# Row maxima turned and loaded in two halves of the heads, scores three slots later, three stacks in place of four

## The reference

```python
h = concat(pos_table, nest_table[nesting(x)], seg_table[segments(x)]) @ W      # (32, 512, 128)
n = layernorm(h)
q, k, v = heads(n @ qkv_w.T + qkv_b)                # 8 heads of 16
h = h + (softmax(q @ k.T / 4) @ v) @ out_w.T + out_b
n = layernorm(h)
g = softmax(n @ gate_w.T) - sigmoid(n @ thr_w.T) / 4
w = where(g >= 0, g, 0); w = w / sum(w)             # 4 experts
h = h + sum_e w_e * (((relu(n @ fc1_e.T) @ loraA_e) @ loraB_e) @ fc2_e.T)
```

## Time and profile before

| | |
|---|---|
| median of three runs | 1129.23 us (1129.39, 1129.23, 1126.67) |
| the profiled execution | 1126.86 us, span 1125.1 us |
| PE busy (matmuls, ends modelled) | 1040.1 us, 92% of the span |
| DVE busy | 948.8 us, 84% |
| ACT busy | 807.0 us, 72% |
| POOL busy | 682.1 us, 61% |
| 1024 maxima tiles on DVE (L1025) | 649.0 us, 679 ns each |
| 1024 exponentials on ACT (L592) | 556.3 us, 600 ns each |
| mean granted TensorE clock | 0.962 of 2.4 GHz |

### The profile page before, as it was taken

One profiled execution on the slowest core, in us unless ns is written; L12 is line 12 of the kernel. 1 busy time (PEld: TensorE's weight loads), 2 busy tenths in 40 slices (PEclk: granted clock), 3 DMA queues, 4 the chain that ended last, 5 costly groups with the idle time before them and its releaser, 6 DMA issues.

```text
span 1125.1 us, 20263 instructions
## 1 busy us (share of the span) xinstructions
PE 1040.1 (92%) x6158; PEld 407.9 (36%) x6158; DVE 948.8 (84%) x2442; ACT 807.0 (72%) x1578; POOL 682.1 (61%) x684
## 2 busy tenths in 40 slices
PE   4368999999999999999999999999999999989865
PEld 2112233333434434343433443434343343333322
DVE  7498899999989989899999999999999998887312
ACT  2217787777877788787877778778787777856731
POOL 1855676677666666677666666667766666621231
PEclk9558999999999999999999999999999999999997
DMA  2553645555554445555555545565555554541111
GB/s 74 148 135 89 137 106 135 129 137 127 137 130 124 126 121 130 142 127 134 126 137 126 126 121 132 130 143 126 137 125 137 128 126 113 121 96 36 55 50 32
DMA packets 93530, 132.43 MB, mean 118 GB/s; under 512 B 18205, under 2 KB 69918, under 8 KB 87398
## 3 DMA queue, kind: packets, MB, share of 16 engines
q1 hardware_dynamic: 91872, 129.54, 47.9%
q10 hardware_dynamic: 1550, 1.59, 0.6%
HBM read 89.20 MB, written 35.01 MB: 110 GB/s over the span
## 4 chain that ended last, share of the span: by engine, by line
PE 64%; DVE 16%; DMA 6%; ACT 5%; issue 2%; POOL 1%; SPq 1%; POOLq 0%; ACTq 0%; DVEq 0%
PE pv L737 17%; PE mix L750 15%; PE sc L724 13%; DVE negmax L1025 9%; PE mix L804 7%; DMA den_dram<-ctx_sb 4%; PE mix L787 3%; DVE bn L1015 2%; ACT probs L592 2%; PE mix L809 2%; DVE h L1050 2%; PE mix L825 2%; DMA den<-den_dram 2%; ACT qk L596 1%; PE mix L769 1%
## 5 line engine op out<-in xcount | busy, mean ns | idle before, releaser
L1025 DVE TENSOR_REDUCE negmax<-mix 128x1 f32<-128x512 f32 x1024 | 649.0, 679 | 56.8 <-PE mix L750 56.2
L592 ACT ACTIVATE probs<-sc 128x512 f32<-128x512 f32 x1024 | 556.3, 600 | 118.2 <-PE sc L724 112.0
L724 PE MATMUL sc<-qstk,kstk 120*128 120x512 bf16 x1024 | 364.2, 382 | 5.6 <-ACT probs L592 4.9
L750 PE MATMUL mix<-kstk,qstk 96*128 96x512 bf16 x1024 | 331.7, 395 | 24.6 <-DMA kstk<-stack_dram 7.3
L737 PE MATMUL pv<-probs,vals 128*32 128x512 f32 x2048 | 244.8, 595 | 0.0
L528 POOL TENSOR_TENSOR ctxh<-ctx_sb,rdenb 128x512 f32<-128x512 f32 x64 | 81.0, 1268 | 245.3 <-DMA rdenb<-rden_dram 244.5
L750 PEld LDWEIGHTS mix<-kstk,qstk 96*128 96x128 bf16 x1024 | 89.4, 98 | 266.5 <-DVE negmax L1025 76.1
L724 PEld LDWEIGHTS sc<-qstk,kstk 120*128 120x128 bf16 x1024 | 100.1, 98 | 107.5 <-ACT probs L592 33.4
L804 PE MATMUL mix<-xn2T,fc1T_sb 128*128 128x512 f32 x256 | 138.2, 622 | 0.7 <-ACT hid L646 0.7
L508 POOL TENSOR_TENSOR qk<-qk,rstdb 128x512 f32<-128x512 f32 x64 | 81.1, 1269 | 57.9 <-DMA rstdb<-rstd_dram 53.4
L737 PEld LDWEIGHTS pv<-probs,vals 128*32 128x32 f32 x2048 | 59.1, 109 | 117.4 <-issue 100.1
(11 more groups left out here) (141 smaller groups left out, 1088.5 us busy)
## 6 DMA issues: line engine op xcount, KB each, us to landing
stack_dram<-pieces SPq DMA_DIRECT2D x192, 128.0 KB
rdenb<-rden_dram SPq DMA_DIRECT2D x64, 256.0 KB
qstk<-stack_dram SPq DMA_DIRECT2D x31, 384.0 KB, 6.6
kstk<-stack_dram SPq DMA_DIRECT2D x31, 384.0 KB, 8.8
rstdb<-rstd_dram SPq DMA_DIRECT2D x32, 256.0 KB, 3.4
wrow<-w_dram SPq DMA_DIRECT2D x32, 256.0 KB
out<-out_sb SPq DMA_DIRECT2D x32, 256.0 KB, 2.6
qstk<-stack_dram SPq DMA_DIRECT2D x31, 256.0 KB, 7.0
```

The costliest lines, as they stand in the source:

```text
L592: act.activation(probs[:, c % 8, i % 2], sc[:, i % RING], ACT.Exp).then_inc(s_exp, 1)
L724: pe.matmul(sc[:, i % RING, :], kstk[0:KROWS, u, h, j * P:(j + 1) * P], qstk[0:KROWS, u, h, :], start=True, stop=True).then_inc(s_score, 1)
L750: pe.matmul(max_bank(m), qstk[0:STK, u, h, j * P:(j + 1) * P], kstk[0:STK, u, h, :], start=True, stop=True).then_inc(s_mxmm, 1)
L1025: dve.tensor_reduce(negmax[:, m // NT, m % NT:m % NT + 1], max_bank(m), AX.X, ALU.max, negate=True).then_inc(s_max, 1)
```

## The change

The maxima of a sequence begin in slot 7 of the step ahead (`MSTART` = 7) and end in slot 6 of the sequence's own step; its score tiles begin in slot 3 (`SSTART` = 3) and end in slot 2 of the next step. The maxima are cut, turned, copied and loaded in two halves of four heads: the first half in slots 15 and 0, the second in slots 7 and 8. `cut_max` is four small operations twice, `turn_max` four matmuls twice (into four groups of partitions of one bank), `copy_mT` four small copies twice. The first half's DMA is issued by ACT, the second's by SP. Embedding, q, k, v, pieces and stacks are made one step less ahead, the stacks are three (`U` = 3), the one-hot rows two. The product of v moves from slot 15 to slot 4 and its copy to slot 5; the one-hot rows (`hot`) move from slot 15 to slot 11. `normalise` on POOL also waits for the gates of the sequence before.

```diff
-KROWS = STK + 3 * NH
+MROWS = 3 * NH // 2
+KROWS = STK + MROWS
-MSTART = 10
+SSTART, MSTART = 3, 7
-U = 4
-HB, H2 = 5, 2
+U, UV = 3, 4
+HB, H2 = 4, 2
 PRODUCTS = [
-    ("project", -2), ("fc1_3", -3), ("embed", 4), ("low", -3), ("none", None), ("xn2T", -2), ("out", -3), ("gates", -2),
-    ("turn_gates", -2), ("fc1_0", -2), ("fc1_1", -2), ("mT", 1), ("q", 4), ("fc1_2", -2), ("k", 4), ("v", 4),
+    ("project", -2), ("fc1_3", -3), ("embed", 3), ("low", -3), ("v", 3), ("xn2T", -2), ("out", -3), ("gates", -2),
+    ("turn_gates", -2), ("fc1_0", -2), ("fc1_1", -2), ("turned", 3), ("q", 3), ("fc1_2", -2), ("k", 3), ("mT", 1),
-BEFORE, BEHIND = (3, 7), (11,)
+BEFORE, BEHIND = (3, 7), (11, 15)
 POOL_FILL = [
-    ("add_bias", 3, 0), ("scale", 3, 0), ("scale", 3, 1), ("rstd1", 4, 0),
-    ("second", 3, 0), ("residual", 3, 0), ("third", 3, 0), ("second", 3, 1), ("residual", 3, 1), ("third", 3, 1), ("v", 3, 0),
+    ("add_bias", 2, 0), ("scale", 2, 0), ("scale", 2, 1), ("rstd1", 3, 0),
+    ("second", 2, 0), ("residual", 2, 0), ("third", 2, 0), ("second", 2, 1), ("residual", 2, 1), ("third", 2, 1), ("v", 3, 0),
...
-            def load_max(b, u):
-                upto(sp, s_mT, b)
-                sp.dma_start(qstk[STK:KROWS, u, :, :],
-                             mT[:].unsqueeze(1).broadcast_to([3 * NH, NH, S])).then_inc(s_mrow, 16)
+            def load_max(b, g, u):
+                upto(sp, s_mT, b, 8, 4 * g + 4)
+                sp.dma_start(qstk[STK:KROWS, u, 4 * g:4 * g + 4, :],
+                             mT[:, g].unsqueeze(1).broadcast_to([MROWS, 4, S])).then_inc(s_mrow[g], 16)
...
+            def normalise(b):
+
+                if b < NSEQ - 1:
+                    upto(pool, s_gate, b - 1, 13)
...
+            def copy_mT(b, g, u):
+
+                upto(act, s_mTmm, b, 2, g + 1)
+                upto(act, s_mrow[g], b - 1, 16)
+                bank = aux(("mT", "gates")[g], 1)
+                for j in range(NT):
+                    act.copy(mT[:, g, j * P:(j + 1) * P], bank[Q * j:Q * j + MROWS, g * P:g * P + P]).then_inc(s_mT, 1)
+                if g == 0:
+                    upto(act, s_mT, b, 8, 4)
+                    act.dma_start(qstk[STK:KROWS, u, 0:4, :],
+                                  mT[:, 0].unsqueeze(1).broadcast_to([MROWS, 4, S])).then_inc(s_mrow[0], 16)
...
+            def turn_max(b, g):
+
+                upto(pe, s_mp, b, 8, 4 * g + 4)
+                bank = aux(("mT", "gates")[g], 1)
                 for j in range(NT):
-                    mm = pe.matmul(aux("mT")[0:3 * NH, j, :], mpc[:, j].rearrange("p a h -> p (a h)"), id16[:],
-                                   start=True, stop=True)
+                    mm = pe.matmul(bank[Q * j:Q * j + MROWS, g * P:g * P + P], mpc[:, g, j].rearrange("p a h -> p (a h)"),
+                                   id16[:], start=True, stop=True)
                 mm.then_inc(s_mTmm, 1)
...
+            def second_half(t):
+
+                if runs(t - 2):
+                    upto(pe, s_gat, t - 2)
+                else:
+                    mix_free(t, 3 * 7 + 1)
+                turn_max(t, 1)
...
+                        if what == "behind" and c == 7 and runs(t):
+                            second_half(t)
-                        if what == "scores" and runs(t):
-                            scores_T(t, 2 * c + i, u)
+                        if what == "scores":
+                            b, v = (t, u) if c >= SSTART else (t - 1, (u - 1) % U)
+                            if runs(b):
+                                scores_T(b, 2 * ((c - SSTART) % SLOTS) + i, v)
...
-            def cut_max(b):
+            def cut_max(b, g):
+
+                nm, n = negmax[:, 4 * g:4 * g + 4].rearrange("p h j -> p j h"), 4 * g
+                upto(dve, s_max, b, 32, 16 * g + 16)
+                upto(dve, s_mTmm, b - 1, 2, g + 1)
+                dve.tensor_copy(mpc[:, g, :, 0, :], nm).then_inc(s_mp, 1)
+                upto(dve, s_mp, b, 8, n + 1)
+                dve.tensor_tensor(mres[:], nm, mpc[:, g, :, 0, :], ALU.subtract).then_inc(s_mp, 1)
+                upto(dve, s_mp, b, 8, n + 2)
+                dve.tensor_copy(mpc[:, g, :, 1, :], mres[:]).then_inc(s_mp, 1)
+                upto(dve, s_mp, b, 8, n + 3)
+                dve.tensor_tensor(mpc[:, g, :, 2, :], mres[:], mpc[:, g, :, 1, :], ALU.subtract).then_inc(s_mp, 1)
```

More of the change, by code:

```diff
@@ L71 @@
     (0, 1, "add_attention", -2, 0), (1, 0, "stats2", -2, 0), (1, 1, "stats2", -2, 1), (2, 0, "moments2", -2, 0),
[L72 to L75, removed]
+    (3, 1, "add_pos", 3, 0), (3, 1, "stats1", 3, 0), (3, 1, "weigh", -3, 0), (6, 0, "stats1", 3, 1),
@@ L76 @@
+    (6, 1, "moments1", 3, 0), (7, 1, "cut", 0, 1), (7, 1, "finish", -3, 0), (7, 1, "invert_den", -1, 0),
+    (9, 0, "gate", -2, 0), (10, 1, "gate", -2, 1), (10, 1, "gate", -2, 2), (10, 1, "gate", -2, 3), (11, 1, "hot", 4, 0),
+    (13, 0, "add_qk", 3, 0), (15, 1, "cut", 1, 0), (15, 1, "add_qk", 3, 1),
 ]
 POOL_WORK = [
-    ("scale", 3, 0), ("add_bias", 3, 0), ("scale", 3, 1), ("rstd2", -2, 0), ("norm2", -2, 0),
-    ("second", 3, 0), ("residual", 3, 0), ("third", 3, 0), ("second", 3, 1), ("rstd1", 4, 0),
@@ L81 @@
-    ("residual", 3, 1), ("third", 3, 1), ("normalise", -1, 0), ("v", 3, 0),
+    ("scale", 2, 0), ("add_bias", 2, 0), ("scale", 2, 1), ("rstd2", -2, 0), ("norm2", -2, 0),
+    ("second", 2, 0), ("residual", 2, 0), ("third", 2, 0), ("second", 2, 1), ("rstd1", 3, 0),
+    ("residual", 2, 1), ("third", 2, 1), ("normalise", -1, 0), ("v", 3, 0),
 ]
 SP_WORK = [
-    ("piece", 3, (0, 0)), ("piece", 3, (1, 0)), ("den_out", -1, 1), ("piece", 3, (0, 1)), ("den_in", -1, 0),
-    ("piece", 3, (0, 2)), ("ids", 5, 0), ("out", -3, 0), ("piece", 3, (1, 1)), ("rden_out", -1, 0), ("piece", 3, (1, 2)),
@@ L309, in steps @@
         def steps(eng, step):
-            for t in range(-5, NSEQ + 3):
+            for t in range(-4, NSEQ + 3):
                 step(t, t % U)
@@ L451, in _ @@
         def _(pool):
-            for v in range(U):
+            for v in range(UV):
                 pool.memset(vals[:, v, :, 0:4, HC:Q], 1.0).then_inc(s_pconst, 1)
@@ L850, in mix_user @@
                     name, ahead = PRODUCTS[c]
-                    if name == "none":
-                        return -1, (s_h, 1, 1)
-                    if name == "mT" and not runs(t + 1):
-                        return (t - 2, (s_wT, 1, 1)) if t > 0 else (t + 4, (s_rT, 1, 1))
+                    if name == "turned":
+                        return (t - 2, (s_wT, 1, 1)) if runs(t - 2) else (t + 3, (s_rT, 1, 1))
+                    if name == "gates" and runs(t):
+                        return t, (s_mT, 8, 8)
                     return t + ahead, products[name][1]
-                return t + (2 if c >= MSTART else 1), (s_max, TILES, 2 * ((c - MSTART) % SLOTS) + kind // 2 + 1)
+                return t + (1 if c >= MSTART else 0), (s_max, TILES, 2 * ((c - MSTART) % SLOTS) + kind // 2 + 1)
             def mix_free(t, n):
@@ L1106, in tile_max @@
             def tile_max(t, c, i):
[L1107 removed]
+                ahead = 1 if c >= MSTART else 0
                 if runs(t + ahead):
```

157 lines of the change are left out of this document (70 added, 87 removed).

## The result

Before 1129.3 us (median of 4), after 1388.5 us (1385.8 to 1390.8, 4 runs): ratio 1.230 [1.227, 1.233]. The forecast was 1138 (1111 to 1152): the sign was right, the size was not near. By the medians 259 us are to be found; the profiled executions, which span 1388.8 and 1125.1 us, differ by 263.7.

What follows compares the result with a forecast made beforehand. VectorE was taken to bound the front, with TensorE at half clock; in the middle both have hardly a gap. From 1126.86 us: front −18.7, end +3.9, middle +25.5 give 1137.6, so 1138 us, range 1111 to 1152.

Steps and rivals of the forecast that it cites:

- its signs of being wrong: Small casts of slot 7 at 0.2 us, projections 31.3 apart; DVE waiting for tiles in slot 7; PE for maxima in slot 3.
- The cut of slot 7: Middle, slot 7: cut ahead of finish, third operation held by POOL's residual until F+1.5; +0.8 us a step (0 to +1.5).
- The cut of slot 15: Middle, slot 15: cut near add_qk's old place, beside POOL's scaling of the values; +0.3 us a step (0 to 0.8).
- Slots 10 to 12, −0.35: Middle: old cut's four DVE operations and four PE matmuls go; −0.35 us a step, bounds −0.85 and 0.
- The rest, +0.1: Middle: v's move, ACT's small copies, landing of the maxima's first half, SP's order, three stacks; +0.1 us a step.
- the middle: Sum of four edits that add to DVE or PE: +0.85 us a step over 30 steps, +25.5 us.
- The front, −18.7: Before slot 3 of step 0: fewer maxima tiles, −21.2 us; sequence 0's first maximum later, +2.5 us.
- my mark: Front's end: score pair of slot 3 of step 0, at 90.70 us before, forecast near 72.0.
- The end, +3.9: Last steps: 26 maxima tiles return, 5.7 us; spilled score tiles 1.3; late products 0.5; 3.6 come back.
- the bulge of steps 28 and 29: End: these steps 3.6 us longer than two full ones, with turn_weights waiting 2.62 us; forecast to come back.
- The hidden cut: Rival, slot 7: the wait for the softmax sums covers the cut; middle 0, 1112 us (1105 to 1123), chance 0.35.
- The rival that gave 1174: Slot 7: any POOL operation holds every cut operation, cut ends near F+3.0; 36 us more, 1174 us, chance 0.04.

Runs made afterwards that it cites:

- the run with the loads in order and the cuts as changed: Changed kernel with SP loading the maxima's first half ahead of stacks, stacks in two halves of heads; cuts, add_qk and v as the change has them: 1188.4 us.
- the run with SP's load first: Changed kernel, but SP instead of ACT issues the load of the maxima's first half, ahead of the stack loads: 1194.5 us.
- the fastest run: Changed kernel with SP's maxima load first, stacks loaded in two halves of heads, v ahead of normalise, both cuts one tile earlier, add_qk earlier: 1115.2 us.
- the run with v and both cuts moved: Changed kernel with SP's maxima load ahead of stacks, POOL's v ahead of normalise, cuts of slots 7 and 15 one tile earlier: 1138.7 us.
- the run with the filled wait: Changed kernel with 20 matmuls ahead of each sequence's first score tile, which overwrites their result: 1348.9 us.

## Why the prediction was wrong

**The step that failed** is one clause: "The first half of the maxima must land between slot 0 and slot 3, in a stretch where the stack loads keep the DMA engines full: 0 to 0.5, taken as near 0.1." The stretch was named, the conflict was seen, and then given a price that no row carried. The nearest rows were the landing times of the stacks themselves in the kernel before (KB of each load, and at the end the median us from issue to landing; the first and the last of the six):

```profile
qstk<-stack_dram SPq DMA_DIRECT2D x31, 384.0 KB, 6.6
...
kstk<-stack_dram SPq DMA_DIRECT2D x33, 128.0 KB, 10.4
```

Against the 4.4 us that a load issued behind the copies has until slot 3, they give a wait of 2 to 6 us, not 0.5. Measured: 4.2 us a step on the mean for the wait (135.7 in 32), and with the clock behind it 7 us (40.80 against 33.66), some 194 us in all. The prediction lists this wait among its signs of being wrong, but no rival had a price or a chance for it, and the range could not hold it.

**The cut of slot 7, +0.8:** right in its mechanism and nearly in its size. The third operation runs to F+1.52 (F is the cut's start, 638.64) where F+1.5 was worked out; the stretch from the values of slot 7 to those of slot 11 grew by 1.10 us in the run with the loads in order and the cuts as changed.

**The cut of slot 15, +0.3:** right in kind, mis-sized: 1.65 us there. I took POOL's phase from one step. In the run with SP's load first the four groups have means of 232, 306, 801 and 391 ns over both places, 3.46 us for two cuts; the cut of slot 7 takes 1.63 of it, so that of slot 15 takes 1.8 on the mean, where 0.7 is the unhindered sum. And I counted the cut against DVE alone; PE's turning waits for it (1.60 us in the row above), and it stands ahead of `add_qk`, for whose bank PE's next tile waits. Moving v away took 1.1 us a step off this place (4.02 to 2.91 from the values of slot 15 to the projection).

**Slots 10 to 12, −0.35:** −0.63 from the values of slot 11 to those of slot 15, between it and the larger bound. **The rest, +0.1:** 0.33 up to the values of slot 7, without the late load. These stretches part the terms only roughly: the old cut, in slot 10, lies in the one that grew by 1.10, and the product of v left slot 15 for slot 4. Their sum doesn't depend on that: even with the load in time the middle would have been 2.45 us a step, not 0.85, and the kernel 1188 us, outside the range.

**The front, −18.7:** the first maximum came at 51.95 (51.6 worked out), the score pair at 73.54 with 3.50 us of wait for the load (72.0). Both are near by luck. The stacks of sequence 0 were issued 1.2 us later than before (43.56 against 42.35), not 2.5, and by the trace PE waited at 51.95 not for them but for ACT's copy of v. And without the late load the pair would have stood at 70.04: the 25 tiles took 0.72 us each, where 0.82 was taken.

```profile
51.95 3.03 PE L762 MATMUL mix<-kstk,qstk 96*128 96x512 bf16 x6 [9.21 <-ACT v L607]
...
73.54 1.03 PE L736 MATMUL sc<-qstk,kstk 108*128 108x512 bf16 x2 [3.50 <-DMA qstk<-mT]
```

But the gain at that mark was not kept. In the fastest run the pair came at 68.90, 21.8 us earlier than before, and the projection of step 2 at 126.11, only 14.2 earlier than before's 140.28. Windows from the mark to that projection, first before, then the fastest run:

```profile
90.70:140.30 49.60, 44.03 (x259) 13.85 (x258) 44.49 (x94) 38.99 (x75) 28.49 (x28) 1.00 0.44 102
```

```profile
68.90:126.10 57.20, 49.64 (x266) 15.24 (x265) 47.06 (x102) 42.26 (x89) 29.66 (x29) 0.91 0.43 104
```

Before, the first six score tiles ran ahead of my mark, from 85.16 on, while PE was still at the lower level, and the clock was up at 90.70. Now the mark is the first score tile, and the stretch at the lower level lies behind it: by an estimate from the two mean clocks, 0.09 of 57 us is 5 of the 7.6 us given back. I had put the mark where the two programs meet in their slots, not where the clock does.

**The end, +3.9:** the four last gaps between projections are 110.69 us before and 114.11 in the fastest run, +3.4. Of the bulge of steps 28 and 29, 2.7 of the 3.6 us went (66.22 before, 63.55 in the fastest run), and with it the wait of `turn_weights`.

**The rivals.** The hidden cut (1112) was the right picture of what the change can be, once its cuts and loads are moved: 1115, with 14.2 from the front in place of 18.7. As it stands, it was not hidden. The rival that gave 1174 was not borne out: beside the four-element power of slot 7 (638.00 to 639.01) the cast took 0.16 us and the subtraction 0.18. By the Trainium skill, page "SBUF — State Buffer", section "Who interferes with whom", a VectorE operation with two SBUF inputs, as the subtraction is, contends with a GpSimd instruction that reads SBUF; in this row the subtraction took no longer than where nothing holds the cut (0.18, its mean in slot 15 of the run with v and both cuts moved).

## What to carry to other kernels

Here a small transfer took the time of what had been issued ahead of it. When a change gives a load a deadline, list all that is issued in the 10 us ahead, on every queue, and price the load by the landing times of those, not by its bytes; if the big transfers can be split so that the part needed first lands first, put the small one ahead of both. A wait of this kind on TensorE is to be priced with the clock behind it (here 5.9 us at 0.53 behind 5 us of standing), and small VectorE operations between tensors in SBUF are to be put where GpSimd idles, not merely where VectorE does.

## What the runs showed of the hardware

In this kernel a second queue was no way round the first. ACT's load of 48 KB, alone on its queue, waited as long behind SP's stacks (135.7 us in all) as SP's own did (137.3). The Trainium skill, page "DMA: Bandwidth & Descriptors", section "Issuing engines are not separate DMA queues", says that transfers started by different engines run on the same 16 DMA engines and interleave; by that the issuer should make no difference, and the runs agree. The same page, section "Queues, rings and completion order", has the DMA engines take turns between queues packet by packet, by which ACT's load would have come through early: here it was no earlier than SP's, 9.5 us from issue to the score tile. The section also says that a completion is signalled only after a DMA engine's earlier writes, across its queues, which would fit; no run here separates when the data landed from when it was signalled. The trace of the step shown adds that the DMA engines were full (mean share 1.01) from 617.0 to 624.0 and at 0.11 from there to 626.7, when PE went on: the last 2.7 us of the wait are hardly a queue of bytes, and what they are stays open.

The clock was at 1.00 up to the wait, at 0.53 in the 5.9 us that followed 5 us of standing, and at 1.00 again in the 7.4 us after those. In the run with the filled wait the projection and the product of slot 1 ran slow behind a wait of 1.53 us for the cut of slot 15 (0.66 from 526 to 531). But in the run with the loads in order and the cuts as changed PE stood 1.60 us at the same place (537.12), and the clock was 1.00 from 500 to 600: the wait alone doesn't bring the fall, and what else did, no run shows.
